# Zeroing a stage's semaphores inside the next stage, by ranges, with one barrier between stages

## The reference, cut to what matters

```python
x = norm(x + attention(x))          # 32 query heads, 8 key heads, rotary, causal softmax
x = norm(x + ternary_ffn(x))        # 512 -> 2048 -> 512, ternary weights, gelu
x = norm(x + linear_attention(x))   # elu features, silu gates, 16 heads
x = norm(x + experts(x))            # 16 experts of which 2 per token, and a shared one
```

## Time and profile before

| what | us |
|---|---|
| median of three runs | 1861.41 (1860.65 to 1864.36) |
| span of the profiled execution, first to last instruction | 1857.5 |
| what lies around that span, by the median | 3.9 |
| TensorE busy in the span | 1612.1 (87%) |
| VectorE, ScalarE, GpSimd busy | 1174.9, 923.7, 544.5 |
| mean granted TensorE clock | 0.947 of full |

### The profile page before, as it was taken

One profiled execution on the slowest core, in us unless ns is written; L12 is line 12 of the kernel. 1 busy time (PEld: TensorE's weight loads), 2 busy tenths in 40 slices (PEclk: granted clock), 3 DMA queues, 4 the chain that ended last, 5 costly groups with the idle time before them and its releaser, 6 DMA issues. The chain is left out here.

```text
span 1857.5 us, 33679 instructions
## 1 busy us (share of the span) xinstructions
PE 1612.1 (87%) x12586; PEld 807.9 (43%) x12586; DVE 1174.9 (63%) x2012; ACT 923.7 (50%) x1624; POOL 544.5 (29%) x551
## 2 busy tenths in 40 slices
PE   2869999668899997799996999787796999999997
PEld 1523333236333333344442455444453556666564
DVE  2448999435699874699974787699452243333277
ACT  3635777425467773677763566355321333333332
POOL 1656544317000011132322222255154111111154
PEclk9979999889899999899997999899898999999999
DMA  6313221100000000375645999643052564646344
GB/s 234 105 52 63 53 53 36 23 1 2 1 2 2 2 2 1 88 133 104 116 83 163 333 355 353 208 149 112 24 109 57 199 248 140 198 147 203 114 125 136
DMA packets 175122, 210.37 MB, mean 113 GB/s; under 512 B 111610, under 2 KB 114904, under 8 KB 172784
## 3 DMA queue, kind: packets, MB, share of 16 engines
q1 hardware_dynamic: 165504, 184.87, 33.5%
q0 software_dynamic: 7344, 20.73, 4.3%
q10 hardware_dynamic: 2112, 2.62, 0.4%
HBM read 193.33 MB, written 56.40 MB: 134 GB/s over the span
## 5 line engine op out<-in xcount | busy, mean ns | idle before, releaser
L709 ACT ACTIVATE attn_prob<-attn_ps_t 128x512 f32<-128x512 f32 x576 | 312.6, 595 | 167.1 <-PE attn_ps_t L663 165.6
L733 DVE TENSOR_REDUCE attn_mx<-attn_ps_s 128x2 f32<-128x1024 f32 (+3 forms) x304 | 342.8, 1162 | 44.5 <-PE attn_ps_s L644 41.2
L2010 PE MATMUL sparse_ps_g<-wgate,sparse_xT 128*128 128x352 f16 x1128 | 186.4, 316 | 3.6 <-DVE sparse_xT L2088 3.6
L676 PE MATMUL attn_ps_o<-attn_prob,V 128*32 128x256 f32 x2304 | 176.9, 393 | 0.8 <-ACT attn_oT L717 0.8
L2010 PEld LDWEIGHTS sparse_ps_g<-wgate,sparse_xT 128*128 128x128 f16 x1128 | 105.6, 99 | 75.2 <-DVE sparse_xT L2088 24.9
L1159 PE MATMUL lin_ps_z<-arena,lin_xT 128*128 128x512 f16 x576 | 135.8, 387 | 0.9 <-DVE lin_relu L1303 0.9
L663 PE MATMUL attn_ps_t<-arena,KT 64*128 64x256 f16 x1152 | 114.2, 277 | 19.4 <-DMA arena<-attn_mT 13.8
L925 PE MATMUL ffn_ps_fc<-wfcT,ffn_xT 128*128 128x512 f16 x512 | 115.2, 384 | 16.2 <-DMA ffn_xT<-ffn_x 16.2
L935 PE MATMUL ffn_ps_y<-wprojT,ffn_hT 128*128 128x512 f16 x512 | 117.4, 389 | 7.9 <-DMA ffn_hT<-ffn_h 7.9
L2120 POOL DMA_INDIRECT xg<-x_d,token x45 | 42.6, 947 | 259.7 <-PE sparse_ps_x L2000 259.7
L644 PE MATMUL attn_ps_s<-KT,arena 64*128 64x512 f16 (+3 forms) x768 | 116.6, 339 | 2.3 <-DVE attn_mx L733 2.3
(11 more groups left out here) (294 smaller groups left out, 3104.7 us busy)
## 6 DMA issues: line engine op xcount, KB each, us to landing
wgate<-gate_d SPq DMA_DIRECT2D x47, 1408.0 KB
wdown<-down_d SPq DMA_DIRECT2D x47, 768.0 KB
lin_sp_raw<-in_L_ffn_w_gate_up_dram SPq DMA_DIRECT2D x56, 352.0 KB, 5.0
gate_d<-lin_sp_parts SPq DMA_DIRECT2D x56, 352.0 KB, 4.7
y_d<-y SPq DMA_DIRECT2D x47, 256.0 KB
down_d<-lin_sp_parts SPq DMA_DIRECT2D x42, 256.0 KB, 4.9
lin_sp_raw<-in_L_ffn_w_down_dram SPq DMA_DIRECT2D x28, 256.0 KB, 5.0
wfcT<-in_L_ffn_w_fc_dram SPq DMA_DIRECT2D x8, 512.0 KB, 4.6
```

The lines of the kernel that those rows point to most:

```text
L676: last = pe.matmul(ps_o[32 * jj:32 * jj + 32, 256 * half:256 * half + 256], V[:, kt, 4 * jg + jj, :], prob[(2 * q + jj // 2) % 4][:, half, ...
L709: act.activation(prob[g % 4][:, par, :, :], ps_t[:, (2 * g + par) % 3, :, :], ACT.Exp, scale=HD ** -0.5).then_inc(exp_done, 1)
L733: dve.tensor_reduce(mx[x % 2][:, c, :, at:at + per], ps_s[:, 2 * (r % 2):2 * (r % 2) + 2, 0:per * n].rearrange("p e (h k) -> p e h k", k=n ...
L2010: last = pe.matmul(ps_g[u][n][rows, :], xT[u][:, a, k, rows], w, start=(k == 0 and i == 0), stop=(k == KC - 1 and i == 2), skip_group_chec ...
```

## The change

`Phase.__exit__` no longer opens a `Block`. It records the ended stage in `Phase.ended`, and gives back the semaphores of the stage before that one. The function `zero_ended` sorts the numbers of the ended stage's semaphores, joins neighbours to ranges, and issues one `sem_clear(range)` for each range. It is called as the first thing in GpSimd's list in each of the nine stage functions (eleven stages). After the last stage `leave_last` makes one `Block` in which GpSimd zeroes the last stage's semaphores.

```diff
+    ended = []
...
+    def zero_ended(self, pool):
+        for f in Phase.ended:
+            numbers = sorted(s.num for s in f.held)
+            first = numbers[0]
+            for n, after_it in zip(numbers, numbers[1:] + [None]):
+                if after_it != n + 1:
+                    pool.sem_clear(range(first, n + 1))
+                    first = after_it
+
     def __exit__(self, *e):
+        for f in Phase.ended:
+            f.sem_ctx.__exit__(*e)
+        Phase.ended = [self]
+        return self.ctx.__exit__(*e)
+
+    def leave_last(self):
         with self.nc.Block() as block:
             @block.gpsimd
             def _(pool):
-                for s in self.held:
-                    pool.sem_clear(s)
-        self.sem_ctx.__exit__(*e)
-        return self.ctx.__exit__(*e)
+                self.zero_ended(pool)
+        for f in Phase.ended:
+            f.sem_ctx.__exit__(None, None, None)
+        Phase.ended = []
...
             @block.gpsimd
             def _(pool):
+                f.zero_ended(pool)          # in each of the nine stage functions
...
         shared_and_combine(nc, m, out)
+        Phase.leave_last(Phase(nc, "end"))
```

More of the change, by code:

```diff
@@ L385, in _ @@
             def _(pool):
+                f.zero_ended(pool)
                 pool.wait_ge(init_done, 3)
```

## The result

The changed kernel runs in 1833.22 us (median of four runs, 1829.03 to 1835.04) against 1861.78: ratio 0.9843, 95% interval 0.9818 to 0.9868. Run again in two later comparisons it gave 0.9856 (0.9830 to 0.9881) and 0.9853 (0.9824 to 0.9882). By the means of all runs, 16 of it and 96 of before, it is 1835.2 against 1863.4 us, 28.2 us faster, uncertain by about 2.3. These means pool comparisons on several chips, between which the mean of before moves from 1862.1 to 1864.7; each comparison alone gives 29.5, 26.3 and 28.9 us. The forecast was 23.4.

A forecast was written before the change was run, and what follows sets the result against it. TensorE was read as close to the bound within stages, with clears between stages delaying the whole core. Savings 22.0 - 0.1 + 1.1 = 23.0 us took 1861.4 to 1838.4; less 0.4 for the clock, 1838.0, range 1833 to 1843.

The forecast's parts named there:

- What bounds the kernel: Whole kernel: eleven stages closed by barriers, plus the pieces between, where the clears lie on the whole core's path.
- step 1: Ten inner boundaries: removing 268 single clears saves 19.8 us and the second barriers 2.2, 22.0 us in sum.
- Step 2: Head of GpSimd's list: range clears cost 0.07 to 0.15 us a stage, hidden except in lin, which pays 0.1 us.
- Step 3: Last Block: 17 clears become one or two ranges with the same barrier, saving 1.1 us.
- Step 5: Removed pieces: no transfer, preparation or code fetch hidden there would make stages late; a short piece costs nothing extra.
- rival D: Stage starts: something was prepared in the pieces, so each stage starts late; between 1838 and 1861, half is 1850; chance 0.05.
- what lies around the span: Outside the profiled span: the median of the runs lies 3.9 us above it, and this part is not touched.
- The clock: Out's entry: TensorE may keep full clock, winning at most 3 us; 0.4 us subtracted as its weight.
- the moe entry: After sparse: TensorE was idle for 2.7 us in all and the clock stayed at 1.00.
- rival B: Stage entries: shorter idle keeps the clock high, 3 us in out, 1.5 each at one or two others; about 1834; chance 0.12.

## Why the prediction was right or wrong

*What bounds the kernel, and step 1.* Right. The second barrier and the single clears were worth 22.0 us in the sum; the pieces, the end's included, went from 23.6 to 0.5, which is 23.1, and steps 1 and 3 together forecast 23.1. Doubling the clears cost what they measure.

*Step 2, the range's cost.* A size was off: 0.07 to 0.15 us a stage were taken, 0.07 to 0.31 measured: 0.26 for one range of 43 in lin, 0.28 for two ranges in out, 0.31 for three in disp, where one or two had been counted on. In lin GpSimd and TensorE are 0.3 us later after the release, not 0.1. The step's reading "paid in full" is not borne out: three profiles of lin are not longer than before, and with 3.1 us more delay lin was 190.2 us.

*Step 3* is right, 1.0 us by the kernel with single clears inside. *Step 5* is right: in every stage of the changed kernel the first engine starts 0.1 us after the only release and no stage is longer by what was removed, so nothing that matters had been hidden in the pieces (rival D). The stall at taken branches of which the Trainium skill speaks ("Runtime: NRT & Kernel Launch", "Instruction fetch mechanics") does not show here. The sentence on what lies around the span was wrong without harm: where a run's time and span are known together they differ by 1.8 us (1829.03 and 1827.2), so the first profiled execution was itself 2 us faster than the median; the difference was taken from the median, and stands.

*The clock.* This is the step that failed, in size and in place. "I subtract 0.4 us of the possible 3 as its weight": beyond the pieces the change gave some 5. And the place was to be out. There the clock was still full when TensorE restarted, in all three profiles, but fell 1.0, 5.5 and 0.7 us after the release and stayed low for 10, 7 and 10 us. The first profile and the second:

```profile
1164.30:1175.70 11.40, 6.90 (x54) 5.11 (x55) 8.72 (x20) 2.93 (x4) 4.36 (x5) 0.55 0.45 146
```

```profile
1172.60:1184.00 11.40, 6.51 (x54) 4.76 (x55) 8.82 (x20) 2.93 (x4) 4.45 (x5) 0.74 0.46 146
```

0.55 and 0.74 against 0.51, and out is as long as before, 124.1 and 124.0 against 123.8 us. The gain that can be located came from qkv1, attn1 and ffn, 3.6 us, which the step dismissed because "the clock is low before the barrier already", and from moe, 1.0. It is low there, but the low stretch ends earlier against the stage's work, and less of the first work runs at 1.2 GHz: the low clock lasted 5.7 to 6.0 us after attn1's restart in three profiles of before, 3.7 to 3.9 in the changed kernel, and 4.5 to 5.1 against 2.8 to 2.9 after ffn's. That these shifts went the good way is luck in part: the doubled clears shortened ffn as much. The step also took the three runs' spread of 3.7 us as noise with no sign; ten boundaries that all moved gave a sum with a sign. And the moe entry, the row on which rival B rested, was one of two outcomes: at the same 2.7 us of idle TensorE the clock fell in two other profiles of before, and moe was 106.9 us; with 1.4 us it fell at the entry in none. The first 3 us of moe in the second profile of before, to hold against the 1.00 of the earlier trace rows:

```profile
1757.70:1760.70 3.00, 2.92 (x11) 1.49 (x12) 0.00 (x0) 0.00 (x0) 0.00 (x0) 0.50 0.02 5
```

Rival B, 1834, with a chance of 0.12, had the right mechanism and nearly the right time, but half or more of its 3 to 6 us was to come from out, which gave nothing: that its number fits is luck. The rule of the Trainium skill ("TensorE: Matmul & The Clock Gate", "Why this matters for your kernels"), to keep TensorE's idle gaps short, agrees with the 5.2 us that filling the pieces gave.

*Open.* How the 5 us divide over the stages, and when a shifted start gains or loses: nothing here forecasts it. In the kernels with TensorE busy in the piece ahead of attn1, attn1 did not come back to 264.5 (265.6, 267.2, 267.2). With extra matmuls elsewhere and attn1's entry as in the changed kernel it was 267.9 once and 264.5 and 264.6 after, so attn1 too can move by 3 us within one kernel. attn0 was anywhere from 292.3 to 299.9 us over all profiles. Whether attn0's mean is shorter too cannot be told from three profiles each.

## What to carry to other kernels

Time between a barrier's release and the next that only one sequencer fills is paid by all engines at one to one; look for it as stretches in which the windows show nothing busy at all, and move such work into the list of an engine that has slack in the next stage. Joined ranges alone gave 18.3 of the 23.1 us. Where removed idle time lies ahead of TensorE's work, allow for more than the time removed, here a fifth more; it is no rule in proportion, since idle time that was doubled cost nothing beyond itself. And check in a profile of the stage's first microseconds that TensorE, not VectorE, is the bound there before trying to win back the clock with extra work.

## What the runs showed of the hardware

- A clear of a range takes 73 ns for 7 numbers and 263 ns for 43, on GpSimd's sequencer; single clears follow each other every 70 or 71 ns, with a longer step now and then, 73 to 74 ns on the mean.
- The clock is not a function of the idle time alone: with TensorE idle for 2.7 us ahead of moe it fell in two profiles of three and stayed in one. And 3.5 us of empty piece ahead of ffn left a stage of 249.4 us where 1.9 us left 250.6 to 251.0.
- More time at the full clock is not less time: 23 us less at the low clock gave nothing where extra matmuls won them back, and some 11 us less in the stages went with 5 us in the changed kernel.
- Stage lengths vary with the clock: one kernel's attn0 is 292.3, 292.4 or 298.4 us with identical instructions, with 36, 36 and 46 us of it at the low clock. The amount alone does not set it: with two pieces filled attn0 was 298.3 us at 35.5.
